# One core, four transformer layers: four full self attentions strung together into one stream of beats

## The chip, the cores and the metric

The kernel runs on one core of one Trainium2 chip. The metric is the device time of one execution in microseconds (us); a measurement is the median of several runs. The core has a matrix engine (TensorE, PE in the profile, with PEld for its weight loads), a vector engine (VectorE, DVE), an activation engine (ScalarE, ACT), GpSimd (POOL), and SyncE (SP), which issues the DMAs here. Each engine works through its own list of instructions in the order in which the program wrote them; between engines they wait on semaphores.

## What is computed

Four layers run over two samples (B = 2) of S = 1024 tokens and C = 256 channels, with 16 heads of 16 channels. Two of the layers, L2 and L3, hold a full self attention, and those are the ones concerned here. L2 has a block mask and rotary positions, L3 has neither:

```python
q, k, v = ...                                   # from layer norm, modulation, one projection
s = jnp.einsum('bqhd,bkhd->bhqk', q, k) * scale # 1024 x 1024 for each head and sample
s = jnp.where(mask, s, jnp.finfo(s.dtype).min)  # L2 only
a = jax.nn.softmax(s, axis=-1)
self_out = jnp.einsum('bhqk,bkhd->bqhd', a, v).reshape(b, s, d) @ attn_out_W
x = x + g_msa * self_out
cross = ...                                     # cross attention over 77 context tokens
x = x + g_x * cross
x = x + g_mlp * (gelu(norm(x) @ mlp_W1 + b1) @ mlp_W2 + b2)
```

The samples do not depend on each other. Within a sample, L3's self attention needs L2's MLP, which needs L2's cross attention, which needs L2's self attention. Layers L0 (windowed attention, a top-16 cross attention, SwiGLU) and L1 (a mixture of three experts) run before.

## The kernel before, in words

Every stage of the work (a norm, a projection, an attention, an MLP) is an object with one small program for each engine, which yields after every **beat**, and with a number of beats. `phases` is a list written by hand. Each phase has lanes, each lane a sequence of stages. `weave` writes out a phase for each engine: one beat of the first lane, then as many beats of the other lanes as keeps them in proportion, until all are through. So the instruction order on every engine is that of the phases and of the beats in them, and a phase's first instruction on an engine stands behind the last one of the phase before.

In the four phases that hold the self attentions the first lane ("lane A", PSUM banks 0 to 4) is nothing but one attention, and the second ("lane D", banks 5 to 7) is a long chain of small stages of the other sample.

An attention runs over 8 groups of 2 heads. In each group the maxima come first: 32 **max tiles** (128 queries x 512 keys, matmul L1044 into bank 0 or 1, then VectorE's maximum, L1167 with L2's mask or L1170 without). The maxima of a group are transposed (L1017), split into two bf16 rows (L1128, L1130) and written by DMA into two rows of the q stack (L996). Then follow 32 **exponential tiles** (matmul L1069 into bank 2 or 3, L2's mask by four more matmuls, L1073, then ScalarE's Exp, L1111), and for every four of them the product with v (L1097, bank 4). At the end the sums are copied (L911), turned (L918) and divided (L929, L934).

In beats, group g starts at `lead + period * g` with lead = 5. A max tile is worked at beats 0 to 31 of its group, an exponential tile at beats 40 to 71, the product with v from 46 on, the copy of the sums at 74 (`lags=(32, 40, 46, 74)`). The period is 40 for L2 (`self2`) and 32 for L3 (`self3`). So inside an attention the maxima of one group stand beside the exponentials of the group ahead of it. An attention has `lead + period * 7 + 74 + 4` beats, 363 in L2 and 307 in L3. Its first 45 beats have no exponentials, and its last 46 no maxima.

The stacks that hold q and k of a group: L2 has two of them (`stacks=(0, 1)`), so group g + 2 is loaded when the last exponential tile of group g has read its stack. L3 has three (0, 1, 2); the third lies in the room of L2's mask and gets its constant rows from GpSimd (`third`, L1907 to L1914) when L2's last attention is through.

```python
def weave(first, *others):
    n = max(sum(n for _, n in first), 1)
    one = beats_of(first)
    lanes = [[beats_of(parts), sum(m for _, m in parts), 0] for parts in others]
    for i in range(n):
        next(one, None)
        for lane in lanes:
            program, m, done = lane
            while lane[2] < (i + 1) * m // n:
                next(program)
                lane[2] += 1
```

Beats of the lane D stages, from their classes: norm of a sample 16, of half of one 10; output projection 14; q or k projection (`Parts`) 10, v projection (`Values`) 9; cross attention 79; L2's or L3's MLP 71; experts of half a sample 95; context 12, context norm 3; `third`, `v_late`, `v_high2`, `query_rows` and the store 1 each.

## Time and profile before

| what | value |
|---|---|
| median of 3 runs | 2946.28 us (2945.03 to 2948.88) |
| the profiled execution | 2955.26 us, its span 2953.9 us |
| mean granted TensorE clock | 0.898 of full speed |
| busy share of the span | PE 83%, DVE 61%, ACT 42%, PEld 42%, POOL 9% |

The span is that from the first to the last instruction of the profiled execution. Matmul ends are modelled in the profile, so a PE that is busy all the time isn't necessarily at its peak. The granted clock is that of TensorE: 1.00 is 2.4 GHz, and 0.5 would be 1.2 GHz all the time; a mean between them is a share of time at each.

### The profile page before, as it was taken

What the parts mean: (1) busy time and instruction counts of PE and PEld (TensorE: products, weight loads), DVE (VectorE), ACT (ScalarE), POOL (GpSimd) and SP (SyncE); (2) the same over time, 40 slices, a digit from 0 to 9 for tenths busy, and PEclk for the clock granted to TensorE, in tenths of its full rate; (3) what the DMA queues carried; (4) which work ended last, traced back from release to release, by engine and by line L of the source; (5) the groups of instructions that cost most, each with busy time, mean ns of one, the idle gap of its engine ahead of it and who ended that gap; (6) DMA issues with size and microseconds to landing.
All of it is one profiled execution on the core that took longest, in us unless ns stands there. A gap on an engine that the chain in (4) does not pass through costs nothing.

```text
span 2953.9 us, 37129 instructions
## 1 busy us (share of the span) xinstructions
PE 2453.4 (83%) x13127; PEld 1253.9 (42%) x13127; DVE 1806.5 (61%) x5631; ACT 1252.9 (42%) x2346; POOL 258.2 (9%) x252
## 2 busy tenths in 40 slices
PE   5777568787798878999788989987889978899678
PEld 2555325454455444444344445442234332234335
DVE  5554857677433466557667666648776667775344
ACT  2323324343222213445335555534646626666334
POOL 2010010010210010000020010010010010000201
PEclk8798689788899887999899999997999989999869
DMA  4545232000000130000232110042220032110120
GB/s 157 153 133 153 74 112 70 12 20 13 8 7 18 43 92 1 23 22 13 88 90 76 34 28 12 12 128 72 60 43 12 33 91 81 41 26 8 56 56 15
DMA packets 151646, 161.30 MB, mean 55 GB/s; under 512 B 33471, under 2 KB 120979, under 8 KB 151197
## 3 DMA queue, kind: packets, MB, share of 16 engines
q1 hardware_dynamic: 151460, 158.94, 18.6%
q8 instruction: 104, 1.70, 0.2%
q14 instruction: 82, 0.66, 0.1%
HBM read 98.04 MB, written 60.19 MB: 54 GB/s over the span
## 4 chain that ended last, share of the span: by engine, by line
PE 61%; DVE 21%; ACT 6%; DMA 5%; issue 3%; POOL 2%; SPq 2%; DVEq 0%; ACTq 0%; POOLq 0%
PE bank L1097 9%; PE bank L1560 7%; PE bank L1069 7%; PE bank L1044 7%; PE bank L1581 5%; PE bank L2034 3%; PE bank L1073 3%; PE bank L722 3%; DVE max L1170 3%; PE bank L1480 2%; PE bank L2211 2%; DVE bank L1167 2%; ACT work L1111 2%; PE bank L663 1%; PE bank L2036 1%
## 5 line engine op out<-in xcount | busy, mean ns | idle before, releaser
L1111 ACT ACTIVATE work<-bank 128x512 f32<-128x512 f32 (+1 forms) x1216 | 700.0, 597 | 631.7 <-PE bank L1073 283.9
L1167 DVE CUSTOM_DVE_ANT_0 bank<-bank,weights 128x512 f32<-128x512 f32 x512 | 349.1, 702 | 199.3 <-PE bank L1044 197.8
L1044 PE MATMUL bank<-k_stack,q_stack 97*128 97x512 bf16 x896 | 368.1, 414 | 79.6 <-DVE max L1167 36.3
L1170 DVE TENSOR_REDUCE max<-bank 128x1 f32<-128x512 f32 x512 | 340.5, 685 | 133.8 <-PE bank L1044 132.0
L1069 PE MATMUL bank<-q_stack,k_stack 99*128 99x512 bf16 x896 | 348.0, 391 | 17.1 <-ACT work L1111 13.9
L1560 PE MATMUL bank<-hT,weights 128*128 128x512 f32 x512 | 265.7, 618 | 17.7 <-ACT work L1606 6.5
L1073 PEld LDWEIGHTS bank<-ident_b,weights 128*128 128x128 bf16 x2048 | 161.1, 99 | 122.5 <-issue 16.3
L1044 PEld LDWEIGHTS bank<-k_stack,q_stack 97*128 97x128 bf16 x896 | 90.6, 101 | 282.7 <-DVE max L1167 107.1
L1073 PE MATMUL bank<-ident_b,weights 128*128 128x128 bf16 x2048 | 202.0, 221 | 0.0
L1581 PE MATMUL bank<-weights,work 128*128 128x256 f32 x768 | 196.4, 384 | 1.0 <-DVE work L1634 1.0
L663 PE MATMUL bank<-ident,work 128*128 128x128 f32 x320 | 84.8, 375 | 118.5 <-DVE work L641 113.1
L1411 POOL TENSOR_TENSOR x<-x,work 128x512 f32<-128x512 f32 x64 | 81.7, 1276 | 1088.4 <-DVE work L1400 1084.1
L722 PE MATMUL bank<-hT,weights 128*128 128x512 f32 x288 | 161.1, 658 | 11.0 <-ACT hT L684 7.9
L1581 PEld LDWEIGHTS bank<-weights,work 128*128 128x128 f32 x768 | 141.0, 190 | 62.5 <-issue 41.2
L1157 DVE TENSOR_REDUCE max<-bank 128x4 f32<-128x308 f32 (+1 forms) x192 | 102.8, 545 | 83.6 <-PE bank L1050 83.2
L1069 PEld LDWEIGHTS bank<-q_stack,k_stack 99*128 99x128 bf16 x896 | 89.4, 100 | 126.6 <-ACT work L1111 67.6
L1097 PE MATMUL bank<-work,v 128*17 128x512 f32 x1024 | 140.7, 622 | 0.0
L1097 PE MATMUL bank<-work,weights 128*17 128x512 f32 x1024 | 136.9, 607 | 0.0
L2034 PE MATMUL bank<-hT,weights 128*128 128x512 f32 (+1 forms) x240 | 133.3, 652 | 3.4 <-ACT work L2228 3.3
L1560 PEld LDWEIGHTS bank<-hT,weights 128*128 128x128 f32 x512 | 90.2, 193 | 99.2 <-issue 62.0
L1284 ACT ACTIVATE k_stack<-bank,top 128x77 f32<-128x77 f32 x256 | 62.1, 328 | 150.6 <-DVE k_stack L1334 150.6
L663 PEld LDWEIGHTS bank<-ident,work 128*128 128x128 f32 x320 | 47.1, 183 | 165.9 <-DVE work L641 133.4
(238 smaller groups left out, 3674.0 us busy)
## 6 DMA issues: line engine op xcount, KB each, us to landing
q_stack<-parts_q SPq DMA_DIRECT2D x60, 384.0 KB, 3.7
parts_q<-parts SPq DMA_DIRECT2D x46, 384.0 KB, 2.5
k_stack<-parts_k SPq DMA_DIRECT2D x40, 384.0 KB, 4.7
weights<-parts_q SPq DMA_DIRECT2D x36, 384.0 KB, 3.6
parts_q<-parts SPq DMA_DIRECT2D x46, 256.0 KB, 2.9
parts_k<-parts SPq DMA_DIRECT2D x24, 384.0 KB, 2.5
parts_k<-parts SPq DMA_DIRECT2D x24, 256.0 KB, 2.9
weights<-in_L_e_w SPq DMA_DIRECT2D x12, 512.0 KB, 5.6
```

The lines of the kernel that those rows point to most:

```text
L663: m = pe.e.transpose(banks[key, bl, c].ap[:, i * P:(i + 1) * P], work[key, "z", t].ap[:, c * P:(c + 1) * P], ident[:, :])
L722: m = pe.e.matmul(bank.ap[:, :], w[:, i, self.col + c * P:self.col + (c + 1) * P], hT[self.b][:, bl, i, :], start=i == 0, stop=i == CC - 1)
L1044: m = pe.e.matmul(bank.ap[:, :], self.q(g)[0:MAX_ROW, h, qt * P:(qt + 1) * P], k_stacks[self.key, g].ap[0:MAX_ROW, h, half * BLK:(half + 1 ...
L1069: m = pe.e.matmul(bank.ap[0:self.nk, :], self.k(g, h, STACK, kt * P), q, start=True, stop=not self.mask)
L1073: m = pe.e.matmul(bank.ap[:, j * P:(j + 1) * P], mask_bias[:, half * TPB + j, kt * P:(kt + 1) * P], ident_b[:, :], start=False, stop=j == ...
L1097: m = pe.e.matmul(o[strip:strip + DV, :], self.v[:, kt, head, :] if self.own else self.v[:, head, :], p[0:self.nk, :], start=kt == 0, stop ...
L1111: ac.e.activation(p.ap[0:self.nk, :], banks[self.key, "exp", g, i].ap[0:self.nk, :], ACT.Exp).then_inc(*probs.tick((self.key, g, i)))
L1167: ve.e.tensor_tensor_reduce(bank[:, :], bank[:, :], mask_bias[:, qt, half * BLK:(half + 1) * BLK], 1.0, -3.4e38, ALU.add, ALU.max, to).the ...
L1170: ve.e.tensor_reduce(to, bank[:, :], AX_X, ALU.max).then_inc(*maxima.tick((self.key, g, i)))
L1560: m = pe.e.matmul(banks[key].ap[:, :], w1[:, k, col:col + P], hT[self.b][:, bl, k, :], start=k == 0, stop=k == CC - 1)
L1581: m = pe.e.matmul(banks[self.key, tp].ap[:, i * C:(i + 1) * C], hid[:, at * P:(at + 1) * P], w2[:, j, :], start=(j == 0 and i == 0), stop= ...
L2034: return pe.e.matmul(out, wt[name][:, k, lo:hi], hT[self.b][:, self.bl, k, :], start=k == 0, stop=False)
```

## The change

The four attentions become one `Stream`. Attention n starts `groups * period` beats after the one ahead of it (at 0, 320, 640 and 896), which is where a ninth group of the one ahead would have started; so the first max tiles of one attention stand beside the last exponential tiles of the one ahead. The stream has 1203 beats, where the four attentions had 363 + 363 + 307 + 307 = 1340. The banks for maxima and exponentials, and the probability buffers, go on counting through the attentions.

The stream is cut into seven `Stretch`es, and each is the first lane of a phase. They are, in beats: 309, 55, 265, 55, 187, 77 and 255. Lane D's stages stand beside them: beside the 309 what stood beside the first attention, without v2 and `query_rows`; beside the first 55 these two; beside the 265 what stood beside the second attention, without v3; beside the second 55 v3; beside the 187 what stood beside the third, again without v3; beside the 77 that; beside the 255 what stood beside the fourth. Lane D itself does the same work in the same order.

The q and k stacks of a new attention's first groups are loaded where the one ahead would have loaded its next group. The third stack is loaded for the first time at beat 45 of the first L3 attention. The second L3 attention takes its stacks in the order 2, 0, 1, and the waits for GpSimd's constant rows go by stack. No stage computes anything else than before.

```diff
-            def stack_free(self, sp, slot):
+            def stack_free(self, sp, slot, i):
                 for f in slot.free:
                     sp.wait_ge(*f)
-                for done, key in self.stacks_free:
+                for done, key in self.stacks_free.get(i, ()):
...
-                n = g * self.n + i
+                n = self.exps + g * self.n + i
...
+                if now := self.group(beat, self.exp_at + self.n, 1):
+                    g = now[0] + self.depth
+                    if g < self.groups:
+                        self.load(sp, g)
+                    elif self.next is not None:
+                        self.next.load(sp, g - self.groups)
...
+        class Stream:
+            def __init__(self, *attentions):
+                self.parts, self.at, self.running, at = attentions, [], {}, 0
+                for n, one in enumerate(attentions):
+                    self.at.append(at)
+                    one.exps = sum(o.groups * o.n for o in attentions[:n])
+                    one.next = attentions[n + 1] if n + 1 < len(attentions) else None
+                    self.beats = at + one.beats
+                    at += one.groups * one.period
+            def active(self, beat):
+                return [(one, beat - at) for one, at in zip(self.parts, self.at) if 0 <= beat - at < one.beats]
+            def first_max(self, n):
+                return self.at[n] + self.parts[n].lead
+            def ended(self, n):
+                return self.at[n] + self.parts[n].beats - 1
+            def tensor(self, pe):
+                turns = counter()
+                for one in self.parts:
+                    one.turns = turns
+                for beat in range(self.beats):
+                    for one, at in self.active(beat):
+                        one.tensor_beat(pe, at)
+                    yield
+            def vector(self, ve):
+                for beat in range(self.beats):
+                    for one, at in self.active(beat):
+                        one.vector_beat(ve, at)
+                    yield
+            def scalar(self, ac):
+                for beat in range(self.beats):
+                    for one, at in self.active(beat):
+                        one.scalar_beat(ac, at)
+                    yield
+            def sync(self, sp):
+                for g in range(self.parts[0].depth):
+                    self.parts[0].load(sp, g)
+                for beat in range(self.beats):
+                    for one, at in self.active(beat):
+                        one.sync_beat(sp, at)
+                        before = self.parts[self.parts.index(one) - 1] if one is not self.parts[0] else one
+                        if at == one.exp_at + one.lead:
+                            for g in range(before.depth, one.depth):
+                                one.load(sp, g)
+                    yield
+        class Stretch(Stage):
+            def __init__(self, stream, first, last):
+                self.stream, self.first, self.beats = stream, first, last - first
+            def go_on(self, name, program, e):
+                s = self.stream
+                if self.first == 0:
+                    s.running[name] = program(e)
+                for _ in range(self.beats):
+                    next(s.running[name])
+                    yield
+            def tensor(self, pe):
+                return self.go_on("tensor", self.stream.tensor, pe)
...
+            turn = ((0, 1, 2), (2, 0, 1))[b]
             st["self3"] = Attention(lane_a, b, "L3", "full", st["q3"], st["k3"], (V, V_late)[b], [(vec, (st["v3"].key, "all"))],
-                                    [(dense, (st["v3"].key, "all"))], rows_ready=k_rows + [("third", 0)], keys_ready=[],
-                                    period=32, stacks=(0, 1, 2), stacks_free=[(pool_done, ("third", 0))], **full_of)
+                                    [(dense, (st["v3"].key, "all"))], rows_ready=[(k_rows + [("third", 0)])[i] for i in turn],
+                                    keys_ready=[], period=32, stacks=turn, stacks_free={2: [(pool_done, ("third", 0))]}, **full_of)
...
+        stream = Stream(one_["self2"], two_["self2"], one_["self3"], two_["self3"])
+        ends = [0]
+        for n, ahead in ((1, 16), (2, 16), (3, 30)):
+            ends += [stream.first_max(n) - ahead, stream.ended(n - 1) + 2]
+        ends.append(stream.beats)
+        stretch = [Stretch(stream, lo, hi) for lo, hi in zip(ends, ends[1:])]
...
-            (of(0, "self2"), of(1, ("e", 1, "n"), ("e", 1)) + [v_high2] + of(1, "n4", "k2", "q2", "v2") + [query_rows],
-             [Rest(30), load_l2m, load_l3]),
-            (of(1, "self2"), of(0, "so2", "n5", "xq2", "cross2", "co2", "n6", "mlp2", "n7", "k3", "q3", "v3")),
-            (of(0, "self3"), [third] + of(1, "so2", "n5", "xq2", "cross2", "co2") + [ctx_norm, context3, v_late]
-             + of(1, "n6", "mlp2", "n7", "k3", "q3", "v3"), [load_l3m, Rest(8)]),
-            (of(1, "self3"), last_0),
+            ([stretch[0]], of(1, ("e", 1, "n"), ("e", 1)) + [v_high2] + of(1, "n4", "k2", "q2"), [Rest(30), load_l2m, load_l3]),
+            ([stretch[1]], of(1, "v2") + [query_rows]),
+            ([stretch[2]], of(0, "so2", "n5", "xq2", "cross2", "co2", "n6", "mlp2", "n7", "k3", "q3")),
+            ([stretch[3]], of(0, "v3")),
+            ([stretch[4]], [third] + of(1, "so2", "n5", "xq2", "cross2", "co2") + [ctx_norm, context3, v_late]
+             + of(1, "n6", "mlp2", "n7", "k3", "q3"), [load_l3m, Rest(8)]),
+            ([stretch[5]], of(1, "v3")),
+            ([stretch[6]], last_0),
```

Below are rows of the programs' own order, with buffer numbers. The line numbers of the changed kernel are a few higher: L1050 is L1044 (max tile), L1075 is L1069 and L1079 is L1073 (exponential tile and its mask), L1103 is L1097 (product with v), L917 is L918, L1026 is L1017, L835 is L834 (v projection), L1000 is L996, L902 is L903.

TensorE where the first attention ends and the second begins, before. L1456 and L1480 are the output projection of the first sample, lane D of the next phase:

```order
L1069 MATMUL bank3<-q_stack1,k_stack1 128x512
L1073 MATMUL bank3<-ident_b,weights 128x128 x4
L834 MATMUL bank6<-weights,hT1 128x256 x2
L1097 MATMUL bank4<-work0,v 17x512
L1097 MATMUL bank4<-work1,v 17x512
L1097 MATMUL bank4<-work2,v 17x512
L1097 MATMUL bank4<-work3,v 17x512
L918 MATMUL bank1<-ident,work7 128x128 x4
L1456 MATMUL bank5<-ident,hT0 128x128 x4
L1456 MATMUL bank6<-ident,hT0 128x128 x4
L1480 MATMUL bank7<-weights,work8 128x256
L1480 MATMUL bank7<-weights,work9 128x256
L1044 MATMUL bank0<-k_stack0,q_stack0 128x512
```

TensorE at the first max tiles of the second attention in the changed kernel; stack 1 still belongs to the last group of the first attention, stack 0 to the first group of the second:

```order
L917 MATMUL bank0<-ident,work7 128x128 x4
L1075 MATMUL bank2<-q_stack1,k_stack1 128x512
L1079 MATMUL bank2<-ident_b,weights 128x128 x4
L1050 MATMUL bank1<-k_stack0,q_stack0 128x512
L835 MATMUL bank7<-weights,hT1 128x256 x2
L1075 MATMUL bank3<-q_stack1,k_stack1 128x512
L1079 MATMUL bank3<-ident_b,weights 128x128 x4
L1050 MATMUL bank0<-k_stack0,q_stack0 128x512
L1075 MATMUL bank2<-q_stack1,k_stack1 128x512
L1079 MATMUL bank2<-ident_b,weights 128x128 x4
L1050 MATMUL bank1<-k_stack0,q_stack0 128x512
L1075 MATMUL bank3<-q_stack1,k_stack1 128x512
```

The last exponential tiles stood ahead of the first max tiles; now they alternate with them, and the output projection has gone behind.

TensorE where the third attention (the first of L3) begins, before, with lane D's output projection beside it:

```order
L1456 MATMUL bank6<-ident,hT1 128x128 x4
L1480 MATMUL bank7<-weights,work8 128x256
L1480 MATMUL bank7<-weights,work9 128x256
L1044 MATMUL bank0<-k_stack0,q_stack0 128x512
L1480 MATMUL bank7<-weights,work8 128x256
L1480 MATMUL bank7<-weights,work9 128x256
L1044 MATMUL bank1<-k_stack0,q_stack0 128x512
```

TensorE in the changed kernel where the last exponential tiles of the second attention (stack 1) end and the second group of the third attention (also stack 1) begins:

```order
L1075 MATMUL bank3<-q_stack1,k_stack1 128x512
L1079 MATMUL bank3<-ident_b,weights 128x128 x4
L1050 MATMUL bank0<-k_stack0,q_stack0 128x512
L1050 MATMUL bank1<-k_stack1,q_stack1 128x512
L835 MATMUL bank6<-weights,hT0 128x256 x2
L1050 MATMUL bank0<-k_stack1,q_stack1 128x512
L1026 MATMUL bank1<-ident,max1_0 16x128
```

Between the last read of stack 1 and the first max tile that needs its new contents stands one other max tile now.

SyncE's queue at the same place, before. It writes the last parts of q, loads all three stacks, and goes on with the next phase:

```order
L805 DMA parts_q0<-parts1 128x3x512
L805 DMA parts_q0<-parts1 128x2x512
L805 DMA parts_q0<-parts1 128x512
L821 DMA row_consts0<-in_L3_b_qkv 128x256
L903 DMA q_stack0<-parts_q0 96x2x1024
L983 DMA k_stack0<-parts_k0 96x2x1024
L903 DMA q_stack1<-parts_q0 96x2x1024
L983 DMA k_stack1<-parts_k0 96x2x1024
L903 DMA weights<-parts_q0 96x2x1024
L983 DMA weights<-parts_k0 96x2x1024
```

The same in the changed kernel (`max_parts` are the two rows of maxima, L1000):

```order
L806 DMA parts_q0<-parts1 128x512
L822 DMA row_consts0<-in_L3_b_qkv 128x256
L902 DMA q_stack0<-parts_q0 96x2x1024
L983 DMA k_stack0<-parts_k0 96x2x1024
L1000 DMA q_stack1<-max_parts0 1x16x128 x2
L902 DMA q_stack1<-parts_q0 96x2x1024
L983 DMA k_stack1<-parts_k0 96x2x1024
L1000 DMA q_stack0<-max_parts0 1x16x128 x2
L902 DMA weights<-parts_q0 96x2x1024
L983 DMA weights<-parts_k0 96x2x1024
L1447 DMA row_consts1<-mod_rows_L2 128x256
```

The load of stack 1 stood right behind that of stack 0; now the rows of maxima of the second attention's last group stand between, and the third stack comes after the rows of the third attention's first group.

## Rows read from the trace of the kernel before

**Rows 1.** The page: TensorE busy and clock, VectorE busy, in 40 slices

```profile
PE   5777568787798878999788989987889978899678
...
DVE  5554857677433466557667666648776667775344
...
PEclk8798689788899887999899999997999989999869
```

**Rows 2.** Windows: the phases of the four self attentions, in order

```profile
core 0: us, PE busy (x) PEld busy (x) DVE busy (x) ACT busy (x) POOL busy (x), PEclk, DMA share, GB/s
1096.00:1523.50 427.50, 381.58 (x2452) 185.18 (x2453) 264.34 (x738) 186.26 (x319) 21.95 (x14) 0.92 0.15 44
1523.50:1970.00 446.50, 404.85 (x2770) 205.30 (x2770) 288.40 (x838) 230.01 (x396) 27.93 (x24) 0.97 0.14 44
1970.00:2393.00 423.00, 364.34 (x1765) 148.68 (x1764) 285.06 (x625) 227.09 (x402) 24.99 (x24) 0.92 0.21 57
2393.00:2760.00 367.00, 325.35 (x1655) 127.17 (x1654) 250.39 (x510) 207.70 (x374) 29.65 (x34) 0.95 0.12 34
```

**Rows 3.** Windows, columns as in rows 2: the three seams, then four full stretches

```profile
1475.00:1564.00 89.00, 71.67 (x397) 36.46 (x396) 57.81 (x157) 27.11 (x48) 15.92 (x10) 0.87 0.25 75
1909.00:2017.00 108.00, 85.95 (x415) 43.19 (x415) 51.98 (x122) 38.04 (x65) 10.45 (x7) 0.83 0.28 88
2329.00:2431.00 102.00, 76.81 (x307) 33.26 (x307) 57.75 (x150) 39.34 (x69) 11.61 (x13) 0.87 0.31 89
...
1564.00:1755.00 191.00, 172.27 (x1386) 85.45 (x1384) 134.42 (x407) 106.28 (x187) 5.07 (x4) 0.99 0.18 53
1755.00:1870.00 115.00, 114.12 (x697) 60.55 (x696) 68.11 (x171) 65.16 (x112) 9.85 (x11) 1.00 0.06 15
2057.00:2142.00 85.00, 75.37 (x485) 24.40 (x483) 61.53 (x133) 55.60 (x102) 0.00 (x0) 0.98 0.21 57
2431.00:2583.00 152.00, 135.29 (x782) 43.55 (x783) 116.05 (x236) 94.26 (x172) 5.80 (x8) 0.96 0.20 59
```

**Rows 4.** Windows, columns as in rows 2: heads of attentions two to four

```profile
1523.50:1564.00 40.50, 28.00 (x90) 13.15 (x90) 32.65 (x110) 4.37 (x7) 5.06 (x4) 0.71 0.00 1
...
1970.00:2017.00 47.00, 32.04 (x88) 15.91 (x87) 30.79 (x75) 4.63 (x8) 5.05 (x4) 0.65 0.14 38
...
2393.00:2431.00 38.00, 24.46 (x79) 11.53 (x77) 30.09 (x73) 2.28 (x4) 11.61 (x13) 0.73 0.10 21
```

**Rows 5.** Waits of TensorE in the second head, 1523.5 to 1564

```profile
PE bank L1044 <- DVE max L1167: 9.0, 12, 1.6
```

**Rows 6.** Timeline of TensorE at the end of the first attention

```profile
1512.48 0.38 PE L1069 MATMUL bank<-q_stack,k_stack 99*128 99x512 bf16 x1
1512.70 0.39 PE L1073 MATMUL bank<-ident_b,weights 128*128 128x128 bf16 x4
1512.93 0.38 PE L1069 MATMUL bank<-q_stack,k_stack 99*128 99x512 bf16 x1
1513.15 0.39 PE L1073 MATMUL bank<-ident_b,weights 128*128 128x128 bf16 x4
1513.46 1.05 PE L1097 MATMUL bank<-work,v 128*17 128x512 f32 x8
1514.45 1.13 PE L834 MATMUL bank<-weights,hT 128*128 128x256 f32 x4
...
1523.11 0.38 PE L1044 MATMUL bank<-k_stack,q_stack 97*128 97x512 bf16 x1
1523.33 1.03 PE L1480 MATMUL bank<-weights,work 128*128 128x256 f32 x4
```

**Rows 7.** Timeline in the second head: VectorE's masked maxima

```profile
1535.45 0.73 DVE L1167 CUSTOM_DVE_ANT_0 bank<-bank,weights 128x512 f32<-128x512 f32 x1
...
1536.10 0.73 DVE L1167 CUSTOM_DVE_ANT_0 bank<-bank,weights 128x512 f32<-128x512 f32 x1
```

**Rows 8.** Timeline: VectorE's unmasked maxima in the third head

```profile
1989.31 1.88 DVE L1170 TENSOR_REDUCE max<-bank 128x1 f32<-128x512 f32 x3
```

**Rows 9.** Timeline: VectorE's shuffle that opens a rotary item, beside max tiles

```profile
1454.00 0.77 DVE L771 STREAM_SHUFFLE work<-work 128x512 f32<-128x512 f32 x1
...
1464.40 0.77 DVE L771 STREAM_SHUFFLE work<-work 128x512 f32<-128x512 f32 x1
```

**Rows 10.** Timeline: the same without max tiles

```profile
1480.53 0.72 DVE L771 STREAM_SHUFFLE work<-work 128x512 f32<-128x512 f32 x1
...
1486.27 0.72 DVE L771 STREAM_SHUFFLE work<-work 128x512 f32<-128x512 f32 x1
```

**Rows 11.** k stack loads, 1096 to 2760: issue to landing

```profile
DMA to landing us min/median/max: 3.9/4.6/10.0
```

**Rows 12.** Waits of TensorE, 1564 to 1755

```profile
PE bank L918 <- ACT work L911: 5.2, 8, 0.9
PE bank L1050 <- DVE hT L934: 3.8, 4, 1.0
```

157 lines of the change are left out of this document (83 added, 74 removed).

## The prediction

> **What bounds the kernel now.** I read the page's slices first: over the second half TensorE stands at 7 to 9 tenths, VectorE at 5 to 7, and the granted clock has dips [rows 1]. No engine is full throughout, so the question is where TensorE is full and where not. Next I cut the time by the four phases that hold a self attention, each from its first max tile to the next one's: 427.5, 446.5, 423.0 and 367.0 us, 1664 us in all, with TensorE busy for 1476 us of them [rows 2]. Then I looked inside. In the full stretches, where maxima, exponentials and lane D run together, TensorE is busy 172.27 of 191, 114.12 of 115, 75.37 of 85 and 135.29 of 152 us, 497 of 543 or 91.5%, at a clock of 0.96 to 1.00 [rows 3]. There TensorE sets the pace. At the three seams, from an attention's last max tile to the end of the next one's head, it is busy 71.67 of 89, 85.95 of 108 and 76.81 of 102 us [rows 3]. The heads (max tiles only, no exponentials) are the worst part: busy 28 of 40.5, 32 of 47, 24.5 of 38 us, and at a mean clock of 0.71, 0.65 and 0.73 [rows 4], so that much of this work ran at 1.2 GHz. VectorE is at 65 to 81% there, and TensorE waits for it: 9.0 us in the second head for a max bank [rows 5]. Tails lack maxima, heads lack exponentials, and the change lays one over the other.
>
> **What the change moves.** No operation is added or taken away. Lane A, from the first attention's start to the last one's end, shrinks from 1340 beats to 1203; lane D has its 920 beats as before (152 + 265 + 282 + 221). So I price a beat. For TensorE the distance from start to start is what counts: an exponential tile takes 0.45 us with its mask and 0.22 without, a max tile 0.22, eight products with v 0.99, so 0.12 per tile [rows 6]. A masked pair is 0.79 us, 0.63 per beat over 32 of 40 beats; an unmasked pair, and beat, is 0.56. VectorE's max takes 0.65 us masked [rows 7] and 1.88/3, about 0.6, unmasked [rows 8], so in a joined stretch with little of lane D the masked pairs hang on TensorE and the unmasked ones on both.
>
> **First account, by beats.** In the four long stretches lane D now stands denser. A lane D beat took 427.5/152 = 2.81, 446.5/265 = 1.685, 423/282 = 1.50 and 367/221 = 1.66 us [rows 2]. It had 2.39, 1.37, 1.09 and 1.39 lane A beats beside it; now 309/142 = 2.18, 265/256 = 1.035, 187/273 = 0.685 and 255/221 = 1.15. If TensorE sets the pace, each lane D beat gets shorter by the lane A work that left it: 0.21 x 0.63 = 0.13, 0.335 x 0.63 = 0.21, 0.40 x 0.56 = 0.23, 0.235 x 0.56 = 0.13 us. The four long stretches then take 142 x 2.68 = 380, 256 x 1.47 = 377, 273 x 1.27 = 348 and 221 x 1.53 = 338 us, 1443 together. Without any shortening it would be 1607, so 164 us hang on this step.
>
> The three joined stretches come on top. The first (55 beats, v2 beside it): 40 masked pairs 32 us, v2 eight times 1.13 = 9 us [rows 6], and about 5 us for the two gaps of 8 beats where rows of maxima and sums go from engine to engine: 46. The second (55 beats, v3) is the same with 8 more max tiles, 47, and a new wait of 6 us (below): 53. The third (77 beats, unmasked, without gaps): 77 x 0.56 = 43, v3 9, and 3 for VectorE, whose 77 x 0.6 = 46 us of maxima and the sums leave it hardly a pause: 55. Together 154. 1443 + 154 = 1597 against 1664: **67 us less**.
>
> **Second account, by the seams.** Their 299 us hold 71.67 + 85.95 + 76.81 = 234.4 us of busy TensorE [rows 3]. With a mean clock c, busy time at half rate is too long by (1 - c) of it: 0.29 x 28.0 = 8.1, 0.35 x 32.0 = 11.2 and 0.27 x 24.5 = 6.6 us in the heads [rows 4]. That leaves 208.5 us of work at full clock. Paid at the 91.5% of the full stretches it is 228 us, 71 less. What this account leaves out is the new wait (6), the gaps in the joined stretches (5 + 5 + 3), and some 5 us for the rotary items of the next paragraph: 47 us less.
>
> **Where something gets longer.** The second sample's rotary k2 and q2 now end at beat 309, beside max tiles all the way except the 8 beats in which no group has tiles. An item takes 10.4 us beside max tiles [rows 9] and 5.75 without [rows 10], because VectorE does seven operations in a row for it, one of them behind GpSimd, while max tiles queue behind these and TensorE behind them. Before, four of eight items stood with max tiles and four without, about 65 us; now about six and two, 74 us. For that the stretch holds 10 more max tiles and less of the experts has them beside it, so 5 us net is what I put down; 0 and 10 are its bounds.
>
> The new wait: the second group of the third attention uses stack 1, which the last exponential tile of the second attention reads to its end. One max tile stands between. The load can only be issued then: two issues and a landing of 4.6 us (3.9 to 10.0) [rows 11], so TensorE stands some 6 us at that max tile, with v3 and everything of both lanes queued behind it. Before, all three stacks were loaded in a row ahead of the attention. Bounds: 4 to 11 us. Elsewhere the period of 40 leaves 8 beats for the load and three stacks leave more: nothing.
>
> **The sum.** The two accounts say 67 and 47 us less. The first assumes that the whole 164 us come off; of this share r the result is 97 - 164 r. The full stretches are at 91.5%, not 100%, so some of lane A's work lies in gaps that lane D's own chains leave, and taking it out frees nothing: r = 0.9 gives 51 less. I take **50 us less**: 2955 becomes about 2905 for an execution like the profiled one, which lies 9 us above the median, and the median becomes **2896**.
>
> **Rivals.**
> - *Half the gain goes into lane D's chains* (r from 0.63 to 0.8). Lane D has one bank each for its cross attention's maxima, exponentials and sums; TensorE already waits at such places, 5.2 and 3.8 us between 1564 and 1755 [rows 12]. Price: 97 - 164 x 0.72 = 21 less, 2925. Against it: in the MLP stretch TensorE has no gaps at all (114.12 of 115) [rows 3]. Chance 0.15.
> - *Slower: lane D sets its own pace.* If a lane D beat keeps its length because each goes PE, DVE or ACT, and back through one bank, then the 153 beats' worth of lean joined stretches are simply added: 1607 + 154 = 1761, 97 more, 3043 at worst. It decides from r = 0.59 down; r = 0.3 gives 48 more, 2994. For it: between 1564 and 1755 lane D, mostly cross attention, leaves TensorE 19 us idle [rows 3], and 79 of each sample's beats are of that kind. Against it: 10% idle can't swallow a removal of 13%. Chance 0.10; within 0.2%, which lies between, 0.05.
> - *The moved work costs nothing.* Lane D's work in the seams is 208.5 less the pairs (25 + 25 + 18), 140 us. Were there room on TensorE in the full stretches, it would vanish in them, and the time would come to 2896 - 140 = 2756. Against it: 114.12 of 115 us busy in the MLP stretch, and where busy can be checked against the pace, tiles start 0.22 and 0.45 us apart without a pause [rows 6]. Chance 0.02. The Trainium skill speaks for it ("Perfetto Trace Analysis", Identifying the Most-Contended Engine): busy time of matmuls is not a measure of how near TensorE is to its peak, weight loads are, and these are at 60.55 of 115 us there [rows 3]; the pace of the tiles in this trace doesn't bear it out as room.
>
> **How the numbers follow.** The main case (r from 0.8 to 1.1, with the bounds of wait and rotary items) has 0.66 and a range of its own of 2866 to 2912. With the rivals' 0.15 on its slow side, 0.10 and 0.05 beyond, 0.02 and another 0.02 below 2864, the range 2864 to 2938 leaves out 0.2. Faster by over 0.2% (6 us, about what a measurement of this kernel can tell from none): 0.66 + 0.15 + 0.02 + 0.02 = 0.85.
>
> **What would show it.** Right: from one attention's last max tile to the next one's first some 5 to 10 us instead of 48.5, 61 and 64 (seam's start to head's start, [rows 3, 4]); no dips of the clock at the second to fourth head; the joined stretches at 46, 53 and 55 us; the long ones at 380, 377, 348 and 338. One wait of TensorE for a k or q stack of 4 to 11 us at the second seam. Wrong: lane D beats at 1.6 us and more in the second stretch, 1.45 in the third, with TensorE's idle time ended by VectorE or ScalarE at lane D's lines; a clock below 0.9 in the joined stretches; or a q2 that ends so late that the first max tile of the second attention waits for its stack with exponentials queued behind it.

## The result, and the profile after

The changed kernel takes 2994.48 us, the median of four runs (2992.74 to 3002.64), beside 2945.66 us of the kernel before (2940.28 to 2948.88, four runs): a ratio of 1.0156, with a 95% interval of 1.0133 to 1.0179. It was to take 2896, within 2864 to 2938. It is 1.6% slower, and outside the range on the side of the second rival.

The profiled execution took 2995.49 us with a span of 2994.2, 40 us more than before's 2953.9. (The medians are 49 us apart and the ratio of 1.0156 is 46 us; the profiled execution of before lay 9 us above its median, so the windows account for 40 us.) The page of the kernel after shows the same work (13127 TensorE instructions in both, 2475.2 us busy where before has 2453.4) and the slices that answer to [rows 1]:

```profile
span 2994.2 us, 37130 instructions
PE 2475.2 (83%) x13127; PEld 1263.9 (42%) x13127; DVE 1815.4 (61%) x5631; ACT 1262.8 (42%) x2346; POOL 257.5 (9%) x252
...
PE   5787568878797879998698899887879898889668
...
DVE  5554857677434565557767665756566767765344
...
PEclk7788689888898878999799999998889899999868
```

I then cut the time as the prediction had: four long stretches with three joined ones between. These are the windows of the kernel after, with the columns of [rows 2]; the last row is the time behind the stream.

```profile
1103.50:1496.00 392.50, 343.15 (x2109) 165.44 (x2108) 251.53 (x704) 162.67 (x276) 20.83 (x13) 0.90 0.13 40
1496.00:1550.00 54.00, 49.27 (x375) 25.72 (x374) 33.42 (x96) 25.12 (x44) 0.00 (x0) 0.98 0.14 41
1550.00:1940.00 390.00, 353.78 (x2401) 182.54 (x2400) 258.76 (x738) 205.89 (x355) 22.87 (x21) 0.97 0.15 45
1940.00:2005.00 65.00, 53.40 (x376) 26.44 (x374) 37.68 (x75) 25.07 (x42) 5.40 (x3) 0.91 0.21 59
2005.00:2378.00 373.00, 309.51 (x1431) 127.53 (x1429) 237.63 (x532) 189.70 (x329) 24.55 (x24) 0.89 0.20 52
2378.00:2463.00 85.00, 75.72 (x364) 24.32 (x361) 56.15 (x102) 46.40 (x82) 6.52 (x9) 0.92 0.15 43
2463.00:2800.00 337.00, 305.66 (x1601) 121.80 (x1600) 220.21 (x458) 206.29 (x368) 22.72 (x25) 0.98 0.12 35
...
2800.00:2994.00 194.00, 135.26 (x594) 82.14 (x592) 84.00 (x228) 65.31 (x112) 30.70 (x36) 0.77 0.17 46
```

The seven rows hold 1696.5 us, where the four of [rows 2] held 1664: 32.5 more. The time behind them is the same, 194 us. The other 7.5 lie ahead of these rows: the first attention starts 3.6 us later, where nothing was moved (its first max tile at 1103.5 instead of 1099.9), and the first row of before was cut 3.9 us ahead of its max tile.

| us | predicted | measured | off by |
|---|---|---|---|
| joined 1, 2, 3 | 46, 53, 55: 154 | 54, 65, 85: 204 | +50 |
| long 1, 2, 3, 4 | 380, 377, 348, 338: 1443 | 392.5, 390, 373, 337: 1492.5 | +49.5 |

Half of the 100 us lies in each. Of the long stretches the third misses by 25 us, the first two by 12.5 and 13, and the fourth not at all (337 for 338). The seams themselves did close: from one attention's last max tile to the next one's first it is 6.2, 7.6 and 0.8 us (1504.3 to 1510.5, 1947.0 to 1954.6, 2408.2 to 2409.0).

**Why a joined pair costs more.** The timeline of TensorE in the third joined stretch of the kernel after (start, duration, engine, line, operation) has four pairs of a max tile (L1050) and an exponential tile (L1075) and then the product with v (L1103):

```profile
2424.85 0.39 PE L1050 MATMUL bank<-weights 97*128 97x512 bf16 x1
2425.08 0.38 PE L1075 MATMUL bank<-q_stack,k_stack 99*128 99x512 bf16 x1
2425.30 0.38 PE L1050 MATMUL bank<-weights 97*128 97x512 bf16 x1
2425.52 0.38 PE L1075 MATMUL bank<-q_stack,k_stack 99*128 99x512 bf16 x1
2426.03 0.39 PE L1050 MATMUL bank<-weights 97*128 97x512 bf16 x1
2426.26 0.38 PE L1075 MATMUL bank<-q_stack,k_stack 99*128 99x512 bf16 x1
2426.63 0.39 PE L1050 MATMUL bank<-weights 97*128 97x512 bf16 x1
2426.85 0.38 PE L1075 MATMUL bank<-q_stack,k_stack 99*128 99x512 bf16 x1
2427.16 1.05 PE L1103 MATMUL bank<-work,v 128*17 128x512 f32 x8
2428.15 0.39 PE L1050 MATMUL bank<-weights 97*128 97x512 bf16 x1
```

VectorE's timeline there; the bracket is the idle time ahead of a group and what ended it:

```profile
2425.28 2.48 DVE L1182 TENSOR_REDUCE max<-bank 128x1 f32<-128x512 f32 x4 [0.83 <-PE bank L1050]
2428.58 1.89 DVE L1182 TENSOR_REDUCE max<-bank 128x1 f32<-128x512 f32 x3 [0.81 <-PE bank L1050]
```

Read the two together. VectorE reduces four tiles in 2.48 us, then stands idle for 0.81, and the next four begin 3.30 us after the first: 0.82 per pair, where the prediction had 0.56. Two things make up the difference.

The first is a miscount. Eight records of the product with v belong to four exponential tiles (four L1097 rows for four tiles in the order ahead of the prediction, two records each), and not to eight. So the product costs 0.99/4 = 0.25 us per tile and not 0.12, and TensorE's starts alone ask for 8 x 0.22 + 0.99 = 2.75 us per four pairs, 0.69 per pair and not 0.56.

The second is the loop, 3.30 against 2.75. VectorE's maxima alone would take 0.62 per pair. The third and fourth max tile start 0.51 and 0.37 us behind the tile ahead of them, not 0.22, because their banks are still being reduced (two banks for maxima). The product with v follows in order, and the next max tile starts only 0.99 us behind it. By then VectorE has emptied both banks. So the costs of the two engines add up in part instead of overlapping: 2.48 of VectorE and 0.8 of waiting for TensorE. The beat's price is the length of that loop and not the larger of two busy times.

**Masked pairs.** They run at TensorE's own pace, with the miscount and hardly more. TensorE's timeline in the first joined stretch has four of them between two products with v, and no v2 among them:

```profile
1516.85 0.39 PE L1050 MATMUL bank<-k_stack,q_stack 97*128 97x512 bf16 x1
...
1519.64 1.05 PE L1103 MATMUL bank<-work,v 128*17 128x512 f32 x8
1520.63 0.39 PE L1050 MATMUL bank<-k_stack,q_stack 97*128 97x512 bf16 x1
```

That is 3.78 us for four, 0.95 per pair. The prediction had 0.79; with the product counted right it is 0.45 + 0.22 + 0.25 = 0.92. In the first joined stretch 32 max tiles took 33.5 us with v2 beside them, in the second 32.6 with v3. A window of the first shows TensorE busy throughout:

```profile
1512.00:1544.00 32.00, 31.97 (x256) 16.82 (x254) 22.11 (x62) 17.86 (x31) 0.00 (x0) 1.00 0.01 2
```

**The stack wait** came as predicted. Waits of TensorE in the kernel after, 1940 to 2005 (sum, count, longest):

```profile
PE bank L1050 <- DMA k_stack<-parts_k: 5.2, 1, 5.2
...
PE bank L1075 <- DMA q_stack<-max_parts: 2.1, 1, 2.1
```

### The profile page after: what moved, and what is told of

Read it like the earlier page. It is cut to its first block, busy times and chain, and to the rows that moved or that the text cites. A ratio compares the mean times of both kernels' runs of the same rounds, so it can differ in the third digit from the quotient of the medians.

```text
span 2994.2 us, 37130 instructions
## 1 busy us (share of the span) xinstructions
PE 2475.2 (83%) x13127; PEld 1263.9 (42%) x13127; DVE 1815.4 (61%) x5631; ACT 1262.8 (42%) x2346; POOL 257.5 (9%) x252
## 3 DMA queue, kind: packets, MB, share of 16 engines
q1 hardware_dynamic: 151460, 158.94, 18.5%
## 4 chain that ended last, share of the span: by engine, by line
PE 62%; DVE 20%; ACT 6%; DMA 5%; issue 3%; POOL 2%; SPq 2%; DVEq 0%; ACTq 0%; POOLq 0%
PE bank L1103 9%; PE bank L1653 7%; PE bank L1075 7%; PE bank L1050 7%; PE bank L1674 5%; PE bank L2127 3%; PE bank L1079 3%; PE bank L723 3%; PE bank L1573 2%; DVE max L1182 2%; PE bank L2304 2%; PE bank L664 2%; DVE bank L1179 2%; DVE k_stack L1427 1%; PE bank L2129 1%
## 5 line engine op out<-in xcount | busy, mean ns | idle before, releaser
L1121 ACT ACTIVATE work<-bank 128x512 f32<-128x512 f32 (+1 forms) x1216 | 707.8, 596 | 754.3 <-PE bank L1075 331.7
L1050 PE MATMUL bank<-k_stack,q_stack 97*128 97x512 bf16 x864 | 352.9, 410 | 74.4 <-DVE max L1179 40.8
L1075 PE MATMUL bank<-q_stack,k_stack 99*128 99x512 bf16 x864 | 340.3, 395 | 7.2 <-DMA q_stack<-max_parts 3.7
L1079 PEld LDWEIGHTS bank<-ident_b,weights 128*128 128x128 bf16 x2048 | 162.7, 100 | 123.5 <-issue 14.1
L1079 PE MATMUL bank<-ident_b,weights 128*128 128x128 bf16 x2048 | 204.0, 223 | 0.0
L1050 PEld LDWEIGHTS bank<-k_stack,q_stack 97*128 97x128 bf16 x864 | 87.9, 102 | 262.0 <-DVE max L1179 102.5
L1103 PE MATMUL bank<-work,v 128*17 128x512 f32 x1024 | 148.0, 653 | 0.0
L1103 PE MATMUL bank<-work,weights 128*17 128x512 f32 x1024 | 140.3, 621 | 1.0 <-DVE weights L860 1.0
L1075 PEld LDWEIGHTS bank<-q_stack,k_stack 99*128 99x128 bf16 x864 | 87.1, 101 | 97.5 <-ACT work L1121 38.4
```

The source lines that it names most:

```text
L1050: m = pe.e.matmul(bank.ap[:, :], self.q(g)[0:MAX_ROW, h, qt * P:(qt + 1) * P], k_stacks[self.key, g].ap[0:MAX_ROW, h, half * BLK:(half + 1 ...
L1075: m = pe.e.matmul(bank.ap[0:self.nk, :], self.k(g, h, STACK, kt * P), q, start=True, stop=not self.mask)
L1079: m = pe.e.matmul(bank.ap[:, j * P:(j + 1) * P], mask_bias[:, half * TPB + j, kt * P:(kt + 1) * P], ident_b[:, :], start=False, stop=j == ...
L1103: m = pe.e.matmul(o[strip:strip + DV, :], self.v[:, kt, head, :] if self.own else self.v[:, head, :], p[0:self.nk, :], start=kt == 0, stop ...
L1121: ac.e.activation(p.ap[0:self.nk, :], banks[self.key, "exp", g, i].ap[0:self.nk, :], ACT.Exp).then_inc(*probs.tick((self.key, g, i)))
```

## The ledger of lane D

For the experiments one more view is wanted: how the time splits for lane D, which alone sets when the next attention's q is ready. From VectorE's timeline of each kernel I took the following marks. A "pause" runs from VectorE's last q part to its first addition of the next output projection, when lane D has only v tiles to do. A runs from the first max tile to the first pause, B and C lie between the pauses, and D runs from the third pause to VectorE's last addition of the output projection behind the fourth attention. For the third pause, the marks of the kernel before and then those of the kernel after:

```profile
2378.72 0.69 DVE L789 TENSOR_TENSOR parts<-work,parts 128x512 bf16<-128x512 f32 x1
...
2397.98 0.69 DVE L1400 TENSOR_TENSOR work<-bank,row_consts 128x512 f32<-128x512 f32 x1 [4.11 <-DMA row_consts<-in_L_b_proj]
```

```profile
2376.64 0.69 DVE L790 TENSOR_TENSOR parts<-work,parts 128x512 bf16<-128x512 f32 x1
...
2468.37 0.69 DVE L1493 TENSOR_TENSOR work<-bank,row_consts 128x512 f32<-128x512 f32 x1 [0.39 <-PE bank L1573]
```

So 19 us before and 92 after. The whole ledger, in us, worked out in this way from the profile of each kernel:

| kernel | A | pause | B | pause | C | pause | D |
|---|---|---|---|---|---|---|---|
| before | 405 | 19 | 427 | 25 | 402 | 19 | 371 |
| after | 389 | 62 | 383 | 72 | 367 | 92 | 341 |
| seam1 | 389 | 64 | 407 | 17 | 398 | 18 | 374 |
| seam12 | 389 | 65 | 384 | 72 | 379 | 18 | 369 |
| seam3 | 404 | 19 | 428 | 19 | 380 | 87 | 345 |
| alone | 404 | 19 | 431 | 275 | 286 | 19 | 373 |
| bank3 | 390 | 64 | 390 | 73 | 366 | 83 | 343 |
| pv_short | 387 | 59 | 386 | 66 | 365 | 85 | 345 |
| late | 389 | 64 | 391 | 74 | 369 | 73 | 343 |
| ctx_lean | 387 | 62 | 385 | 74 | 342 | 98 | 345 |
| all_fix | 390 | 64 | 384 | 72 | 355 | 90 | 345 |
| bank33 | 390 | 70 | 385 | 77 | 376 | 90 | 349 |
| seam1_bank33 | 390 | 70 | 407 | 24 | 399 | 25 | 368 |
| seam1_ctx2 | 392 | 66 | 408 | 17 | 398 | 18 | 369 |
| ctx2_only | 394 | 56 | 432 | 25 | 403 | 18 | 368 |

From before to after the pauses grow by 43, 47 and 73 us, 163 together, and the long stretches give back 16, 44, 35 and 30, 125 together. That leaves 38 more. Each row is one profiled execution. Where kernels have the same order, their entries still differ: B is 427 to 432 in before, seam3, alone and ctx2_only, and 383 to 391 in after, late, ctx_lean and all_fix. So a few us in one entry are no finding. All that follows asks why so much is paid and so little comes back.

## The experiments

### One seam at a time: seam1, seam3, seam12

seam1 joins the two masked attentions alone and leaves the rest as before, seam3 joins the two unmasked ones alone, and seam12 joins the first three. The edit of seam1 (the others are built alike):

```diff
-        stream = Stream(one_["self2"], two_["self2"], one_["self3"], two_["self3"])
+        stream = Stream(one_["self2"], two_["self2"])
...
-        for n, ahead in ((1, 16), (2, 16), (3, 30)):
+        for n, ahead in ((1, 16),):
...
-            ([stretch[2]], of(0, "so2", "n5", "xq2", "cross2", "co2", "n6", "mlp2", "n7", "k3", "q3")),
-            ([stretch[3]], of(0, "v3")),
+            ([stretch[2]], of(0, "so2", "n5", "xq2", "cross2", "co2", "n6", "mlp2", "n7", "k3", "q3", "v3")),
```

> Only the two L2 attentions are joined (a stream of two); the two of L3 stand apart as before. Theory A (joined stretches): a joined stretch has hardly any lane D work, and a pair of tiles takes 1.0 us there, so lane D pauses for 62 instead of 19 us at this seam (+43), and wins back about 16 us in the first long stretch and, with 1.37 lane A beats for each of its own cut to 1.20, about 22 in the second: 5 us slower than before, with the joined stretch at 54 us as in the changed kernel. Theory B (lane D's own chains set the pace of the long stretches, and all seams cost alike, a third of the 40 us each): 13 us slower.

> Only the two L3 attentions are joined; those of L2 stand apart as before. Theory A: lane D's pause grows from 19 to 91 us (+72), because this joined stretch has 77 beats and not 55; against it about 22 us come back in the stretch ahead and 31 in the one behind: 19 us slower than before. Theory B: 13 us slower, like every seam.

> The first three attentions are joined, the fourth stands apart as before. Theory A: two pauses grow by 43 and 47 us, and 16, 43 and about 14 us come back in the long stretches: 17 us slower. Theory B: two thirds of 40, 27 us slower.

Measured: seam1 2947.39 us, ratio 0.9997 (0.9975 to 1.0018); seam12 2958.53, 1.0025 (1.0005 to 1.0046); seam3 2976.91, 1.0090 (1.0063 to 1.0117). Taken as steps, the first seam costs nothing that can be told, the second some 0.3%, and the third, by seam3, 0.9%, or from seam12 to all four 1.3%. (The second step is as large as its error, and the second seam wasn't joined by itself.) In us that is -1 (-7 to +5), +7 (1 to 14) and +27 (19 to 35) for seam1, seam12 and seam3. Theory A had +5, +17 and +19, theory B +13, +27 and +13: A's figures for seam1 and seam3 lie at the edge of the intervals, its third one and all three of B's outside. In the ledger the first seam pays 45 us and gets 16 from A and 20 from B back, with 8 more at the second pause (which seam3, unchanged up to there, has at 19 as well, so hardly the seam's doing); the third pays 68 and gets 22 and 26. The unmasked seam is the bad one: its joined stretch was the longest (77 beats) and its pairs were priced too low by the most (0.82 for 0.56, where masked ones are at 0.95 for 0.79).

### Each lane by itself: alone

The kernel before, with the third attention's phase cut in two: first the attention with no lane D beside it, then the same lane D work with no attention.

```diff
-            (of(0, "self3"), [third] + of(1, "so2", "n5", "xq2", "cross2", "co2") + [ctx_norm, context3, v_late]
-             + of(1, "n6", "mlp2", "n7", "k3", "q3", "v3"), [load_l3m, Rest(8)]),
+            ([third] + of(0, "self3"), [load_l3m, Rest(8)]),
+            (of(1, "so2", "n5", "xq2", "cross2", "co2") + [ctx_norm, context3, v_late]
+             + of(1, "n6", "mlp2", "n7", "k3", "q3", "v3"),),
```

> The kernel before, with the third attention and lane D's chain of the second sample one after the other and not side by side; nothing is left out. It measures the two prices in dispute by themselves. The price that the prediction used for a lone pair of unmasked tiles, 0.56 to 0.6 us, gives the attention 307 beats at about 0.6 = 185 us; theory A says that VectorE's maxima and the product with v follow each other (4 x 0.6 + 0.83 us for four pairs) and gives 0.82 us and more, 250 to 320 us. For lane D alone, 282 beats: if TensorE set its pace, 0.8 us a beat, 225 us; if its own chains do (theory B), 1.2 us and more, 340 us and up.

One run, 3098.44 us. Windows of this kernel: the attention's full part, lane D, and lane D's cross attention:

```profile
2017.00:2196.00 179.00, 165.65 (x843) 41.96 (x843) 133.75 (x239) 118.85 (x209) 0.00 (x0) 1.00 0.11 29
...
2233.00:2530.00 297.00, 195.11 (x680) 103.06 (x679) 117.61 (x318) 82.90 (x136) 25.58 (x24) 0.69 0.20 52
...
2270.00:2360.00 90.00, 57.06 (x255) 21.39 (x258) 25.68 (x70) 23.00 (x39) 0.00 (x0) 0.50 0.18 53
```

VectorE's timeline in the attention, and its waits from 1975 to 2230:

```profile
2154.44 2.48 DVE L1170 TENSOR_REDUCE max<-bank 128x1 f32<-128x512 f32 x4 [0.81 <-PE bank L1044]
...
2157.74 0.69 DVE L1170 TENSOR_REDUCE max<-bank 128x1 f32<-128x512 f32 x1 [0.81 <-PE bank L1044]
```

```profile
DVE max L1170 <- PE bank L1044: 48.0, 61, 3.7
```

The loop of 3.30 us stands here too (2154.44 to 2157.74), with nothing of lane D about. It belongs to the attention and was there before; beside lane D it was hidden, since in [rows 2] an attention beat of the third phase has 423/307 = 1.38 us anyway. It is 28.4 us for 32 pairs with the sums, 0.89 per beat. The third joined stretch by this price is 77 x 0.89 = 68.5 and 9 for v3, 78 us; the prediction said 55, the trace 85. From its first max tile to the first addition behind it the attention took 256 us (1977.1 to 2233.3), within the 250 to 320 of theory A.

The other half of the answer is C. Lane D's 272 beats take 286 us alone, at a clock of 0.69, and 402 with the attention. Set against how many lane A beats stand beside one of lane D:

| kernel | lane A beats per lane D beat | C, us | us per lane D beat |
|---|---|---|---|
| alone | 0 | 286 | 1.05 |
| after | 0.685 | 367 | 1.35 |
| seam3 | 0.846 | 380 | 1.40 |
| seam12 | 0.93 | 379 | 1.39 |
| before | 1.09 | 402 | 1.48 |

From before to after the slope is 0.13/0.405 = 0.32 us per lane A beat, from before to alone 0.43/1.09 = 0.39 (with a lower clock in alone). The prediction let a lane A beat that leaves give back its 0.56 us times 0.9; TensorE's starts in such a beat are 0.69. A lane D beat of 1.05 us alone lies between the 0.8 of a lane that TensorE paces and the 1.2 and more of theory B. So in this stretch much of lane D's pace is its own. That holds for C. In D the lane A beats that left gave back all that they were priced at (337 us for 338), and no run has the lane D work of A, B or D by itself.

### Shortening the loop of a joined pair: bank3, pv_short, bank33

bank3 gives the max tiles a third bank in the joined stretches (lane D's 5, and v2 and v3 go on 6 and 7):

```diff
+                        one.max_banks = (0, 1, 5) if lean and True else (0, 1)
```

> The changed kernel, but in its three joined stretches the max tiles go round three PSUM banks (0, 1 and lane D's 5) and v2 and v3 use only 6 and 7. Theory A (a pair costs 0.82 us because VectorE runs dry behind each product with v: four maxima of 0.6 us and then 0.8 us of nothing): with a third bank TensorE is a tile further ahead when the product starts, VectorE keeps its maxima going, and about 0.5 us per four pairs comes back, over some 160 pairs 20 us: joined stretches from 54, 65 and 85 us to about 48, 60 and 75, the kernel at 2975. Rival (the pace of the joined stretches is one of latencies from engine to engine that a bank doesn't shorten): no change, 2995.

Measured: 2996.96 us, 1.0142 (1.0097 to 1.0187), against the 1.0156 of the change: no difference that can be told, where theory A had 20 us. Four pairs take 3.15 us in its trace instead of 3.30, and the third pause 83 instead of 92; the gain is not seen in the time. ScalarE's timeline in it, and TensorE's weight load for an exponential tile, show who waits now:

```profile
2424.83 1.08 ACT L1121 ACTIVATE work<-bank 128x512 f32<-128x512 f32 x2 [0.65 <-PE bank L1075]
...
2426.79 2.22 ACT L1121 ACTIVATE work<-bank 128x512 f32<-128x512 f32 x4 [0.88 <-PE bank L1075]
```

```profile
2427.44 0.10 PEld L1075 LDWEIGHTS bank<-q_stack,k_stack 99*128 99x128 bf16 x1 [0.59 <-ACT work L1121]
```

With a third bank for VectorE, TensorE's weight load stands 0.59 us until ScalarE frees a bank. So ScalarE's banks hold TensorE up once VectorE's are loosened; bank33 below loosens both, but takes a bank from v as well.

pv_short shortens the link between them: in the joined stretches the product with v takes only the upper halves of v and of the exponentials as bf16. Two lines of it:

```diff
+                            vv = vv.bitcast(BF16).rearrange("p (n two) -> p n two", two=2)[:, :, 1]
+                            pp = pp.bitcast(BF16).rearrange("p (n two) -> p n two", two=2)[:, :, 1]
```

> The changed kernel, but in its three joined stretches the product with v reads only the upper halves of its float32 words, as bf16: a quarter of TensorE's passes, with less exact numbers; nothing else is changed. Theory A: the product is what VectorE's maxima wait behind, 1.0 us for four pairs, and it falls to about 0.25: 0.7 us per four pairs, about 28 us over the three stretches, the joined stretches at 47, 57 and 70 us, the kernel at 2967. Rival (TensorE has slack there): no change, 2995.

Measured: 2976.06 us, 1.0080 (1.0053 to 1.0107). By the ratios that is 0.76% less than the change, 22 us, of the 28 us forecast. TensorE's timeline of this kernel:

```profile
2405.26 0.41 PE L1107 MATMUL bank<-work,v 128*17 128x512 bf16 x4
2405.59 0.39 PE L1050 MATMUL bank<-weights 97*128 97x512 bf16 x1
```

The next max tile starts 0.33 us behind the product instead of 0.99. VectorE's timeline just behind it:

```profile
2406.02 2.48 DVE L1186 TENSOR_REDUCE max<-bank 128x1 f32<-128x512 f32 x4 [0.18 <-PE bank L1050]
2408.67 0.69 DVE L1186 TENSOR_REDUCE max<-bank 128x1 f32<-128x512 f32 x1 [0.16 <-PE bank L1050]
```

Four pairs take 2.65 us and not 3.30: the 0.66 us that the product is shorter come off the loop in full, and VectorE hardly stands. So the product with v, in the line of TensorE where VectorE waits for it, is a link of the loop, and half of the slowdown (0.76 of 1.56%) goes with it. (TensorE's own work gets shorter by the same 0.66 us. For the unmasked pairs the loop was longer than TensorE's starts; for the masked ones, which TensorE paces, the gain is the shorter work itself. The run doesn't tell the two apart in the total.)

bank33 gives three banks to each side (0, 1, 5 and 2, 3, 6), which leaves v2 and v3 bank 7 alone.

```diff
                         one.max_banks = (0, 1, 5) if lean and True else (0, 1)
+                        one.exp_banks = (2, 3, 6) if lean else (2, 3)
```

> The changed kernel with three banks in turn for max tiles (0, 1, 5) and three for exponential tiles (2, 3, 6) in the joined stretches; v2 and v3 have bank 7 alone. With a third bank for maxima only, four pairs went from 3.3 to 3.15 us, and TensorE then waited for ScalarE at the exponential tiles. Theory A, mended (both side engines run dry behind the product with v, because TensorE can be only two tiles ahead of each): four pairs at some 2.8 us, about 0.5 us less, 15 to 20 us over the three stretches, the kernel at 2977. Rival (latencies): 2995.

Measured: 3009.92 us, 1.0213 (1.0182 to 1.0245), slower than the change by 0.6%, where theory A had 15 to 20 us less. TensorE's timeline and its waits between 2380 and 2470:

```profile
2435.46 2.08 PE L835 MATMUL bank<-weights,hT 128*128 128x256 f32 x4 [2.29 <-DVE weights L860]
```

```profile
PE bank L835 <- DVE weights L860: 5.5, 3, 2.3
```

The v tiles on one bank now stall TensorE, each with both lanes behind it. This run mixes two causes and doesn't say what three banks on each side would bring by themselves. seam1_bank33 is the same with the first seam alone:

> Only the two L2 attentions joined, with three banks each for max and exponential tiles in that joined stretch (v2 has bank 7). The kernel with this seam alone came to 0.9997 of before, with a pause of lane D of 64 us where 19 were. Theory A: 40 pairs at 0.13 us less each, about 5 us, 0.998 of before. Rival (latencies): 1.000.

Measured: 2968.77 us, 1.0058 (1.0033 to 1.0082), against 0.9997 of seam1: 0.6% worse for the banks here as well, and neither theory had that. Its first pause is 70 us instead of 64.

### Shortening the joined stretch, and filling it: late, ctx_lean, all_fix

late starts the fourth attention's maxima 12 beats later, so that the third joined stretch has 65 beats and not 77:

```diff
-        for n, ahead in ((1, 16), (2, 16), (3, 30)):
+        for n, ahead in ((1, 16), (2, 16), (3, 18)):
```

> The changed kernel with its third joined stretch cut from 77 beats to 65: lane D's k3 and q3 may end 18 beats ahead of the fourth attention's first max tile and not 30, and the load of that attention's first stack is issued 12 beats later. Theory A: 12 beats leave the stretch in which one costs 1.0 us and go where one costs about 0.4 us beside lane D (the C stretch: a lane D beat takes 1.07 us alone, 1.34 with 0.685 lane A beats, 1.50 with 1.09): 7 us faster than the changed kernel, 2988. Theory B (lane D's chain sets everything): it ends its k3 and q3 as late as before, so 0. If the load comes too late: up to 5 us slower.

Measured: 2986.77 us, 1.0116 (1.0079 to 1.0152). The third pause falls from 92 to 73 us, 19 for 12 beats. The ratio falls by 0.40%, 12 us, which isn't clear of noise by itself: the intervals of late and of the change overlap (theory A had 7 us, theory B none). C, which takes up the 12 beats, is at 369 and not 367. (B is at 391 and not 383, but it lies ahead of the edit, so that is scatter between executions.)

ctx_lean moves lane D's context norm and context from C, which lane D sets, to the third joined stretch, which it doesn't:

```diff
-            ([stretch[4]], [third] + of(1, "so2", "n5", "xq2", "cross2", "co2") + [ctx_norm, context3, v_late]
+            ([stretch[4]], [third] + of(1, "so2", "n5", "xq2", "cross2", "co2") + [v_late]
...
-            ([stretch[5]], of(1, "v3")),
+            ([stretch[5]], of(1, "v3") + [ctx_norm, context3]),
```

> The changed kernel with the context norm and the context projections of L3 (15 lane D beats that only the last cross attentions need) moved from the fifth stretch to the third joined one, beside v3. Theory A: the long stretch loses 15 beats at about 1.1 to 1.37 us, and the lean one has engines to spare and grows by half of that at most: 8 to 15 us faster than the changed kernel, 2980 to 2987. Theory B, that a joined stretch's length is TensorE's work: it grows by what the other loses, 0.

Measured: 2983.32 us, 1.0114 (1.0071 to 1.0157), 12 us less than the change by the ratios, again with intervals that overlap (theory A had 8 to 15). C goes from 367 to 342 us, and the pause only from 92 to 98: the joined stretch did have room for lane D's work.

all_fix has both edits:

> The changed kernel with both mends of its third joined stretch: 65 beats and not 77, and the L3 context stages beside v3. They gave about 11 and 12 us by themselves. Theory A: both hold together, less what the fuller stretch costs: 18 to 23 us faster than the changed kernel, 2972 to 2977. Theory B: nothing more than one of them, 2983.

Measured: 2984.13 us, 1.0124 (1.0096 to 1.0152), no better than either (theory B). TensorE's timeline in this kernel shows one long wait in the pause, and below it is the longest one of ctx_lean:

```profile
2400.18 0.38 PE L1078 MATMUL bank<-q_stack,k_stack 99*128 99x512 bf16 x1
...
2409.42 0.61 PE L1053 MATMUL bank<-weights 97*128 97x512 bf16 x1 [8.86 <-DVE hT L933]
```

```profile
2400.50 0.61 PE L1050 MATMUL bank<-weights 97*128 97x512 bf16 x1 [7.31 <-DVE max L1182]
```

The context norm is a chain of small operations on VectorE, with the maxima queued behind it. A max tile stood 8.86 us for it here, with everything of TensorE behind, and 7.31 us in ctx_lean, which has the same chain and came out no worse. So the chain is a price of filling the stretch, and not the reason why the two edits don't add up. By the ledger they fall short in two places. Added up they would give C 344 and the pause 79 us; it has 355 and 90. The 11 us in C lie ahead of the context norm, and what causes them wasn't found.

### The version that came out ahead: seam1_ctx2, ctx2_only

If a joined stretch pays only when lane D's work fills it, then the cheap seam should be joined and given work. seam1_ctx2 is seam1 with the second layer's context moved from the phase ahead of the attentions to the joined stretch beside v2:

```diff
-        context2 = Context(lane_a, "L2", "L2k", 0, "L2v", 0, None, None, [],
+        context2 = Context(lane_d, "L2", "L2k", 0, "L2v", 0, None, None, [],
...
-            ([stretch[1]], of(1, "v2") + [query_rows]),
+            ([stretch[1]], of(1, "v2") + [query_rows, context2]),
```

> Only the two L2 attentions joined, and L2's context projection (12 lane D beats) moved from the phase ahead of the first attention into the joined stretch, beside v2. Theory A (a joined stretch has engines to spare, a full one hasn't): the phase that loses it gets 10 to 15 us shorter, the joined stretch 3 to 6 longer: about 8 us faster than before, 0.997. Theory B (what is moved costs the same wherever it stands): 1.000.

> The kernel before, no seam joined, with L2's context projection (12 lane D beats) moved from the phase ahead of the first attention to the end of lane D beside the first attention. It tells whether the 0.28% of the kernel with one joined seam and this move came from the move alone. Theory A (a full stretch charges the moved beats in full, a joined one hardly): the phase ahead gets some 10 us shorter and the attention's phase as much longer, 1.000 of before. Rival (the move pays by itself, since that phase had the context projection last and alone behind its other lane): 0.997, and the joined seam had no part in it.

seam1_ctx2: 2939.62 us over 12 runs, ratio 0.9972 (0.9955 to 0.9989). It is the one kernel faster than the kernel before, by 0.28%, as theory A had it (0.997). Its joined stretch:

```profile
1490.00:1550.00 60.00, 56.19 (x403) 30.50 (x404) 37.65 (x112) 27.13 (x48) 0.00 (x0) 0.93 0.29 63
```

The first pause is 66 us where seam1 had 64, so the context costs 2 us there. ctx2_only has the context at the end of lane D beside the first attention, with no seam joined: 2969.04 us, 1.0040 (1.0016 to 1.0064). A and its pause grow from 424 to 450, more than the phase ahead gets shorter (11 us, by the first max tile at 1088.7 and not 1099.9). So the move costs 0.4% without the joined stretch, which neither theory had, and the 0.28% isn't the moved context's alone. Of the gain over seam1 alone (0.9972 against 0.9997, in different sets of runs) the intervals say less: they overlap.

## Why the prediction was wrong

**The step that failed first** is the price of a pair in a joined stretch: "In a joined stretch with little of lane D" an unmasked pair was put at 0.56 us, because TensorE's starts need 0.56 and VectorE's maxima 0.6, and the larger of two sets the pace. The trace shows 0.82 without the sums and alone 0.89 with them. Half of the gap is the miscounted product with v, 0.12 us per tile where its records give 0.25: TensorE's starts need 0.69. The other half is the loop: TensorE works in order and runs at most two banks ahead, so VectorE's 2.48 us for four tiles and its 0.8 us behind the product with v are paid one after the other. The three joined stretches took 54, 65 and 85 us and not 46, 53 and 55: 50 us. With the product counted right they would have been put at 51, 58 and 65. So the miscount is 20 of the 50 us. It explains 5 of the first stretch's 8 and 5 of the second's 12 (2.1 more there are a wait for a q stack that the prediction didn't have). In the third it explains 10 of 30. The loop and the sums, at the 0.89 per beat of the attention alone, bring that stretch to 78, and 7 us stay unexplained.

**The step that failed second** is the share r. The working "1607 − 164 r" stood, but with 1492.5 us in the long stretches r is 114.5/164 = 0.70, not 0.9: 33 us. The miscount is in the 164 too. A lane A beat is 0.92 x 0.8 = 0.73 and 0.69 us, not 0.63 and 0.56, so some 196 us hung on this step, and r of that is 0.58. It isn't one number either: in the prediction's own terms 7 of 18.5 us came back in the first long stretch, 41 of 54 in the second, 36.5 of 63 in the third and 30 of 29 in the fourth. For the third the table over alone, after, seam3, seam12 and before is the evidence: 0.32 to 0.39 us per lane A beat taken out.

By its r of 0.70 the outcome lies in the first rival's 0.63 to 0.8, which would have been faster by 18 us; the second rival began at 0.59. Its figure of 2994 for r = 0.3 is the measured median, but by chance, since r wasn't 0.3 and the joined stretches weren't 154. Nor did its signs come: lane D beats took 1.52 and 1.37 us in the second and third stretch (390/256, 373/273), not 1.6 and 1.45. The reason that both rivals name, lane D's own chains, is borne out in part for the third stretch. The second rival's argument against, "10% idle can't swallow a removal of 13%", read idle time off busy time: lane D alone leaves TensorE 102 of 297 us idle, and beside the attention that slack was filled and didn't show as such.

**Both were needed.** The sum with the joined stretches at 204 is 147 − 164 r. With r = 0.9 it is nothing (−1), with r = 0.7 it is 32; and with the old 154 and r = 0.7 it would have been 18 less. The windows gave +32.5. (Counted from the first max tile in both kernels it is 36 and r 0.68; 3.6 us more lie ahead of it, where the change does nothing.) The sum was right that two terms of 150 us and more stand against each other; the range took r alone as uncertain and gave the joined stretches a price without bounds. That is the flaw of the working, more than the chance of 0.10. The miscount by itself did little harm to the sum, since it stands on both sides: with it mended the same working gives 1607 + 174 - 1664 = 117 less 196 x 0.9, 59 us less and not 51. What then is missing is 62 us of r and 30 of the joined stretches.

**Busy time as evidence.** "497 of 543 or 91.5%" was the ground for saying that TensorE sets the pace. In the third joined stretch it is busy 75.72 of 85 us, 89%, while its starts need 77 x 0.69 = 53 and 9 for v3, 62; alone it is busy 165.65 of 179, 93%, with 0.69 of each 0.82 us in use. A busy row counts a matmul until its modelled end and doesn't tell a paced engine from a full one. The Trainium skill (page "Perfetto Trace Analysis", Identifying the Most-Contended Engine) says that the busy share of matmuls is not a good measure of how near TensorE is to its peak, and names the share of peak arithmetic and the weight loads' share instead. The trace agrees here: weight loads are 24.32 of 85 us in this stretch, and 60.55 of 115 in the MLP stretch of before [rows 3]. The prediction had it against one stretch, [rows 6], where tiles do start without a pause, and took that for the rest.

**What was right.** The seams closed (6.2, 7.6 and 0.8 us between last and first max tile). The stack wait was one wait of 5.2 us, within 4 to 11. The last long stretch took 337 us, predicted 338. The eight rotary items of the first took 77 us from the first shuffle to the last q part (1415.2 to 1492.5), predicted 74; but by the same marks before held 74 (1431.2 to 1505.3) and not the 65 of the prediction, so they grew by 3 us.

**The clock.** No dips were expected at the second to fourth head. The joined stretches have 0.98, 0.91 and 0.92, where the heads had 0.71, 0.65 and 0.73 [rows 4]: most of that is gone. In C it is 0.89, and it was 0.92 before; over that stretch's cross attention 0.87 (2058.5 to 2173.7) where before had 0.96 (2029 to 2145). Lane D alone runs at 0.69, and for 90 us of cross attention at 0.50, TensorE's 1.2 GHz. So the clock fell where lane A was thinned beside lane D's cross attention, which would work against the gain. How much of r is the clock and how much lane D's chains through single banks wasn't separated.

**Still open.** Whether more buffers for both side engines would mend the joined pairs, since bank33 took a bank from v as well. How the missing part of r splits between clock and chains in the third stretch, and why so little came back in the first and all in the fourth. And what cost all_fix 11 us ahead of its joined stretch.

## What to carry to other kernels

When work of one lane is packed closer to free a stretch of it, price the packed pair by the loop that it runs in (the in-order engine, the buffers that it may be ahead, the longest link in its queue), best from a run of that lane alone, and not as the larger of the two engines' busy times. Price what is given back elsewhere from two runs with different density: in C 0.32 to 0.39 us came back of a beat that held 0.69 of TensorE's starts, and in D the whole price. Count a product's records against the tiles that they serve before dividing: eight served four here. And laying two halves of one lane over each other leaves the other lane's share of that stretch empty: fill it from a place where that lane sets the time (seam1_ctx2, ctx_lean), or don't join. A serial chain on the side engine has its price there too (waits of 7.31 and 8.86 us in ctx_lean and all_fix).

## What the runs showed of the hardware

The product with v from 4-byte values holds up the next tile by 0.99 us (eight records), and from bf16 by 0.33 us (four). The granted clock was 0.50 over 90 us of lane D alone (2270 to 2360 of alone) although TensorE counts as busy for 57.06 of them; that is its level of 1.2 GHz throughout. And one and the same kernel, the one before, had medians from 2945.66 to 2956.22 us in different sets of runs, so the small differences above are told by ratios within a set.
